# A chain of attention, expert and feed-forward layers on one core: attention-value product ahead of the last score unit, a DRAM fill in 22 pieces, norms in fused instructions, expert choice in three steps

## What is computed

```python
x = x + tanh(g_xattn[0]) * attention(layernorm(x), ctx, ctx)            # att0: 16 heads of 8, 512 keys
x = x + tanh(g_ffn[0])   * moe_top1(layernorm(x))                       # 8 experts, one per token, hidden 512
h = layernorm(x)
y = ln(h + attention(h, h, h), ln1_g, ln1_b)                            # att1: 256 keys
y = ln(y + attention(y, ctx, ctx), ln2_g, ln2_b)                        # att2: 512 keys
y = ln(y + relu(y @ fc1 + b) @ fc2 + b, ln3_g, ln3_b)                   # feed-forward
x = x + tanh(g_xattn[1]) * y
z = layernorm(x)
u = z + causal_attention(rmsnorm(z, g1), rope)                          # att3: 256 keys, 4 key heads
x = x + tanh(g_ffn[1])   * (u + moe_top2(rmsnorm(u, g2)))               # 4 experts, two per token
```

## Time and profile before

| | us |
|---|---|
| Median of three runs | 1365.55 |
| The three runs | 1375.97, 1365.55, 1359.68 |
| The profiled execution's own time | 1377.16 |
| Its span, first to last instruction | 1375.2 |
| TensorE busy | 1138.4 |
| VectorE busy | 789.1 |
| ScalarE busy | 593.9 |
| GpSimd busy | 391.3 |

### The profile page before, as it was taken

How to read it: one execution, slowest core, us unless ns; L and a number is a source line. 1 busy time by engine, 2 the same in 40 slices (tenths; PEclk the granted TensorE clock), 3 DMA queues, 4 the chain that set the end, 5 groups by cost and what they waited for, 6 DMA issues and landing times. The chain is left out here.

```text
span 1375.2 us, 24810 instructions
## 1 busy us (share of the span) xinstructions
PE 1138.4 (83%) x8548; PEld 674.0 (49%) x8548; DVE 789.1 (57%) x1887; ACT 593.9 (43%) x947; POOL 391.3 (28%) x1038
## 2 busy tenths in 40 slices
PE   2799889799888677787899988888888778788897
PEld 1245444377454465344444444434565556555554
DVE  2567776533766212567777758667575655534433
ACT  1266554445564333455455644534443333332121
POOL 2333222611344312454333324222242422100000
PEclk9999887799997789789899998988999988889999
DMA  8544333454335343556444434423343434201000
GB/s 229 152 120 134 113 111 112 148 160 120 96 115 163 94 135 106 148 152 208 152 146 146 144 98 126 130 84 97 93 138 109 144 100 135 63 17 39 8 23 8
DMA packets 173235, 158.72 MB, mean 115 GB/s; under 512 B 12681, under 2 KB 147209, under 8 KB 173065
## 3 DMA queue, kind: packets, MB, share of 16 engines
q1 hardware_dynamic: 168920, 142.02, 34.7%
q0 software_dynamic: 4192, 15.12, 3.5%
HBM read 91.56 MB, written 67.63 MB: 116 GB/s over the span
## 5 line engine op out<-in xcount | busy, mean ns | idle before, releaser
L1043 ACT ACTIVATE prob<-e_ps 128x1024 f32<-128x1024 f32 (+1 forms) x384 | 375.1, 988 | 233.6 <-PE e_ps L1555 157.3
L1202 DVE TENSOR_REDUCE nmax<-s_ps 128x1 f32<-128x512 f32 x512 | 331.5, 685 | 175.4 <-PE s_ps L1518 173.9
L1518 PE MATMUL s_ps<-Kst,Qst 72*128 72x512 bf16 x512 | 207.6, 422 | 68.0 <-DVE nmax L1202 51.1
L1555 PE MATMUL e_ps<-Qst,Kst 75*128 75x256 bf16 x1408 | 252.3, 295 | 13.2 <-DMA Qst<-mrow 4.6
L1571 PE MATMUL av_ps<-prob,Vx 128*32 128x256 f32 (+1 forms) x3072 | 229.1, 422 | 0.0
L1555 PEld LDWEIGHTS e_ps<-Qst,Kst 75*128 75x128 bf16 x1408 | 135.2, 104 | 124.9 <-issue 72.8
L967 POOL TENSOR_TENSOR mparts<-nmax,zeros 128x8 bf16<-128x8 f32 x128 | 26.7, 208 | 376.6 <-issue 363.9
L1571 PEld LDWEIGHTS av_ps<-prob,Vx 128*32 128x32 f32 x3072 | 87.0, 118 | 90.9 <-issue 59.2
L1046 ACT ACTIVATE OT<-av_ps 128x256 f32<-128x256 f32 x128 | 49.2, 384 | 179.6 <-PE av_ps L1571 179.5
L1211 DVE TENSOR_REDUCE nmax<-s_ps 128x2 f32<-128x512 f32 x128 | 85.2, 686 | 59.0 <-PE s_ps L1532 58.6
L1518 PEld LDWEIGHTS s_ps<-Kst,Qst 72*128 72x128 bf16 x512 | 52.9, 104 | 129.0 <-DVE nmax L1202 80.7
(11 more groups left out here) (193 smaller groups left out, 1679.5 us busy)
## 6 DMA issues: line engine op xcount, KB each, us to landing
q_parts<-qp SPq DMA_DIRECT2D x96, 192.0 KB, 2.4
k_parts<-kp SPq DMA_DIRECT2D x48, 384.0 KB, 3.3
Qst<-q_parts SPq DMA_DIRECT2D x128, 144.0 KB
Kst<-k_parts SPq DMA_DIRECT2D x64, 288.0 KB
k_parts<-kp SPq DMA_DIRECT2D x48, 192.0 KB, 2.6
Kst<-k_parts SPq DMA_DIRECT2D x64, 144.0 KB
ctxT<-in_ctxT SPq DMA_DIRECT2D x16, 256.0 KB, 4.6
FB<-xs_rows SPq DMA_DIRECT2D x22, 128.0 KB, 2.5
```

Of the source, the lines that this page charges most:

```text
L1043: act.activation(dst, src, ACT.Exp).then_inc(e_drained, 1)
L1202: ve.tensor_reduce(nmax[:, g, u, h % GH:h % GH + 1], s_ps[:, c % 2, :], AX.X, ALU.max, negate=True).then_inc(s_drained, 1)
L1518: last = pe.matmul(s_ps[:, c % 2, :], Qst[0:ROWS, par, s, u * P:u * P + P], Ks[0:ROWS, par, s, :], start=True, stop=True)
L1555: last = pe.matmul(o, Ks[0:KROWS, par, h, t * P:t * P + P], Qst[0:KROWS, par, h, :], start=True, stop=not a.rope)
```

## The change

1. **Order of the product.** In `body`, the AV piece of a slot stands ahead of the slot's last S unit instead of behind it (in slots with two units: E, first unit, small step, AV, second unit).
2. **Positions.** In att3 `maxT` goes from positions 5 and 9 to 4 and 8, `proj` from 11 to 10, `apply` from 14 to 12, and `v` from 10 to 12. In att1 and att2 `apply` is divided: `center` at 10 and the rest at 13, where it stood at 12.
3. **Norms.** (x - mean)*gain and then *rstd + shift, each one `scalar_tensor_tensor` per 128 x 128 tile; in att3 and `f.rms` x*rstd*gain in one. For att1 and att2 the first pair doesn't need `rstd`, so `center` runs before it is there. In the feed-forward `f.center` and `f.scale` replace `f.norm`, `f.gain` and `f.shift`.
4. **Choice.** `m0.choose` has three parts, at positions 5, 6 and 7 (for the last sequence of a half all at 12).
5. **Fill.** The zeros go out in 22 DMAs of 128 KB, at every second position from position 4 of problem 1 to position 14 of problem 3. The load of `m0c` goes from the start to position 5 of problem 0, with a semaphore of its own.

```diff
     it = {6: [("ctx", n, 0)], 7: [("ctx", n, 1)], 15: [("nT", n, None)]}
     if a.wo:
         it[8] = [("aT", n, None)]
-        it[11] = [("proj", n, None)]
-        it[14] = [("apply", n, None)]
+        it[10 if a.rope else 11] = [("proj", n, None)]
+        it[12 if a.rope else 14] = [("apply", n, None)]
     else:
         it[8] = [("resid", n, None)]
-        it[12] = [("apply", n, None)]
+        it[10] = [("center", n, None)]
+        it[13] = [("apply", n, None)]
...
-        put(n, 15, ("f.norm", i, None))
-        put(n + 1, 0, ("f.gain", i, None))
-        put(n + 1, 1, ("f.shift", i, None))
+        put(n, 15, ("f.center", i, None))
+        put(n + 1, 0, ("f.scale", i, None))
-        put(n + 1, 10, ("f.gain1", i, None))
...
+    put(0, 5, ("m0.const", 0, None))
+    for k in range(2 * NT):
+        put(1, 4 + 2 * k, ("m0.fill", k // NT, k % NT))
     for b in range(B):
         if b % HALF < HALF - 1:
-            for p, kind in ((3, "m0.gate"), (6, "m0.choose"), (9, "m0.rank")):
-                put(b + 2, p, (kind, b, None))
+            put(b + 2, 3, ("m0.gate", b, None))
+            for k in range(3):
+                put(b + 2, 5 + k, ("m0.choose", b, k))
+            put(b + 2, 9, ("m0.rank", b, None))
     for g in range(B // HALF):
         last = HALF * g + HALF - 1
         n = last + 1
-        for p, kind in ((11, "m0.gate"), (12, "m0.choose"), (13, "m0.rank")):
-            put(n, p, (kind, last, None))
+        put(n, 11, ("m0.gate", last, None))
+        for k in range(3):
+            put(n, 12, ("m0.choose", last, k))
+        put(n, 13, ("m0.rank", last, None))
...
-    put(5, ("maxT", n, 2))
-    put(9, ("maxT", n, 3))
+    put(4 if a.rope else 5, ("maxT", n, 2))
+    put(8 if a.rope else 9, ("maxT", n, 3))
...
-        put(10, ("v", n + 1, None))
+        put(12 if a.rope else 10, ("v", n + 1, None))
...
+        product = []
         if s >= a.gs:
-            units += [[("AV", n, (s // a.gs - 1, x))] for x in range(a.avs) if (x + 1) * a.gs // a.avs - 1 == s % a.gs]
+            product = [("AV", n, (s // a.gs - 1, x)) for x in range(a.avs) if (x + 1) * a.gs // a.avs - 1 == s % a.gs]
         elif n > lo:
             p = att(n - 1)
-            units += [[("AV", n - 1, (NG - 1, x))] for x in range(p.avs) if (x + 1) * a.gs // p.avs - 1 == s]
+            product = [("AV", n - 1, (NG - 1, x)) for x in range(p.avs) if (x + 1) * a.gs // p.avs - 1 == s]
+        if product:
+            units.insert(max(1, len(units) - 1), product)
...
+                elif kind == "m0.const":
+                    sp.dma_start(m0c[:, :], dram["m0c"]).then_inc(m0c_loaded, 16)
+                elif kind == "m0.fill":
+                    sp.dma_start(xs_rows[n][arg * TILE:(arg + 1) * TILE, :], dram["blank"]).then_inc(blank_stored, 16)
...
-            late(m0c[:, :], dram["m0c"])
             late(fc1b[:, :], dram["fc1b"])
             late(gw1[:, :], dram["gw1"])
-            for g in range(B // HALF):
-                blank = dram["blank"].unsqueeze(0).to_broadcast([NT, TILE, D])
-                sp.dma_start(xs_rows[g].rearrange("(n r) d -> n r d", r=TILE), blank).then_inc(blank_stored, 16)
...
-                    po.wait_ge(blank_stored, 16 * B // HALF)
+                    po.wait_ge(blank_stored, 16 * 2 * NT)
...
-                    act.wait_ge(late_loaded, LATE)
+                    act.wait_ge(m0c_loaded, 16)
...
+            def center_gain(L, dst, src, gain, t):
+                for i in range(t):
+                    ve.scalar_tensor_tensor(out=dst[:, i, :], in0=src[:, i, :], scalar=L["mv"][:, i, 0:1],
+                                            in1=vecs[:, VI[gain], :], op0=ALU.subtract, op1=ALU.mult)
+            def scale_shift(L, dst, src, shift, t):
+                for i in range(t):
+                    last = ve.scalar_tensor_tensor(out=dst[:, i, :], in0=src[:, i, :], scalar=L["rstd"][:, i:i + 1],
+                                                   in1=vecs[:, VI[shift], :], op0=ALU.mult, op1=ALU.add)
+                return last
+            def scale_rms(L, dst, src, gain, t):
+                for i in range(t):
+                    last = ve.scalar_tensor_tensor(out=dst[:, i, :], in0=src[:, i, :], scalar=L["rstd"][:, i:i + 1],
+                                                   in1=vecs[:, VI[gain], :], op0=ALU.mult, op1=ALU.mult)
                 return last
...
-            def one_hot(dst, src, e, tiles):
+            def one_hot(dst, src, e, tiles, part=None):
...
+                if part in (None, 0):
+                    ve.tensor_reduce(top, src, AX.X, ALU.max)
+                    ve.drain()
+                    ve.tensor_tensor(eq, src, top.unsqueeze(2).to_broadcast(bc), ALU.is_equal)
+                    ve.drain()
+                if part in (None, 1):
+                    ve.tensor_tensor(eq, eq, io, ALU.mult)
+                    ve.drain()
+                    ve.tensor_reduce(low, eq, AX.X, ALU.min)
+                    ve.drain()
+                if part in (None, 2):
+                    ve.tensor_tensor(dst, low.unsqueeze(2).to_broadcast(bc), io, ALU.is_equal)
+                    ve.drain()
...
+                elif kind == "center":
+                    ve.drain()
+                    center_gain(LA, tmp[:, 0:SQ].rearrange("p (t d) -> p t d", t=QT), newres[:, par, :, :],
+                                a.name + "_g", QT)
...
-                        t4 = tmp[:, SQ:2 * SQ].rearrange("p (t d) -> p t d", t=QT)
-                        apply_norm(LA, t3, newres[:, par, :, :], QT, rms=a.tail == "rms")
-                        ve.drain()
                         if a.tail == "rms":
-                            ve.tensor_tensor(dst, t3, over("att3_g", QT), ALU.mult).then_inc(norm_ready, 1)
+                            scale_rms(LA, dst, newres[:, par, :, :], "att3_g", QT).then_inc(norm_ready, 1)
                         else:
-                            ve.tensor_tensor(t4, t3, over(a.name + "_g", QT), ALU.mult)
-                            ve.drain()
-                            ve.tensor_tensor(dst, t4, over(a.name + "_b", QT), ALU.add).then_inc(norm_ready, 1)
+                            scale_shift(LA, dst, t3, a.name + "_b", QT).then_inc(norm_ready, 1)
...
-                    one_hot(ohs[:, j:j + QT, :], lg[:, 0:QT, :], E0, QT)
-                    ve.tensor_copy(ohb[:, :, :], ohs[:, j:j + QT, :]).then_inc(m0_chosen, 1)
+                    one_hot(ohs[:, j:j + QT, :], lg[:, 0:QT, :], E0, QT, arg)
+                    if arg == 2:
+                        ve.tensor_copy(ohb[:, :, :], ohs[:, j:j + QT, :]).then_inc(m0_chosen, 1)
...
-                elif kind == "f.norm":
+                elif kind == "f.center":
+                    ve.drain()
+                    center_gain(LF, f_res, f_res, "ffn_g", BT)
+                elif kind == "f.scale":
                     ve.wait_ge(f_rstd, f_stat(n, 0))
-                    apply_norm(LF, f_res, f_res, BT)
-                elif kind == "f.gain":
-                    ve.drain()
-                    ve.tensor_tensor(f_res, f_res, over("ffn_g", BT), ALU.mult)
-                elif kind == "f.shift":
-                    ve.drain()
-                    ve.tensor_tensor(f_res, f_res, over("ffn_b", BT), ALU.add)
+                    ve.drain()
+                    scale_shift(LF, f_res, f_res, "ffn_b", BT)
...
-                    apply_norm(LF, f_out, f_res, BT, rms=True)
-                elif kind == "f.gain1":
-                    ve.drain()
-                    ve.tensor_tensor(f_out, f_out, over("g1", BT), ALU.mult).then_inc(f_normed, 1)
+                    scale_rms(LF, f_out, f_res, "g1", BT).then_inc(f_normed, 1)
```

23 lines of the change are left out of this document (6 added, 17 removed).

## The result

| | before | changed |
|---|---|---|
| Median of four runs, us | 1370.76 | 1332.86 |
| Lowest and highest, us | 1359.68, 1378.32 | 1320.61, 1336.79 |
| Profiled execution: time, span, us | 1377.16, 1375.2 | 1336.79, 1335.0 |

The changed kernel is faster: ratio 0.9698, 95% interval 0.9645 to 0.9751. The forecast was 1307 us in a range of 1270 to 1350, a ratio of 0.957: the sign and the case are right, the gain is some 38 us instead of 58. A median takes in all executions of a kernel, a ratio and its interval only those within 1.5% of the fastest of the same kernel, so a ratio can differ from the quotient of two medians.

A forecast was written before the change was run, and what follows sets the result against it. TensorE was taken to lose about 237 us in gaps and to run 270 us at half speed. Fill 7.5, 31.4 for choice, product and att3, and clock 20 gave 58.9 us, a factor 0.957: 1307 us, range 1270 to 1350.

The forecast's parts named there:

- The fill, 7.5 us: At the start: without the zeros ahead of the k stores, K's reload and all behind it come 7.5 us earlier (4 to 10.4).
- The choice, 7.8 us: Spreading the choice over three slots closes two TensorE waits of 1.9 us and four of about 1: 7.8 us (3 to 11).
- The product, 13.2 us in att2 and 3 each in att0 and att1: AV ahead of the last unit pays where VectorE has a burst before that unit: 19 us in all (0 to 25).
- a plain pair gains nothing: Two att2 slots without small steps but `maxT`: after the product moves, the wait is as long, only elsewhere.
- 0.85 of the 1.65: Per att2 problem, E comes 0.85 us earlier at slots 10 and 11 because AV starts before the unit that waited.
- att3, 15 us: New att3 positions save 1.2 us in five light problems and 3.1 in three with a choice: 15 us (-12 to 24).
- Three quarters: A closed wait partly opens at the next resource, so 31.4 of the 41.8 us of choice, product and att3 were kept.
- the last three terms: Choice 7.8, product 19 and att3 15 us, together 41.8 us before the reduction to 31.4.
- The clock, 20 us: TensorE: 45 of 270 us at half speed go, mostly behind choices and long `nT` waits, at 0.45 each: 20 us (-20 to 60).
- The signs: Expected in the trace: first unit at 32 to 34 us, no 1.88 us wait, units' waits about 35, clock 0.92 or more.
- The product pays nothing: Rival: moving AV only puts the same wait in another place; 25.5 us gained in all, 1340 us; chance 0.22.
- two-tensor operations in SBUF: Rival: each fused norm operation takes twice 348 ns, costing 20 us on VectorE in its busiest slots: 1327 us; chance 0.02.

The follow-up runs named there:

- the version with the big fill: Changed kernel with the zeros in two DMAs of 1.44 MB, issued at positions 4 and 6 of problem 1, instead of 22 small ones: 1338.5 us, ratio 0.9751.
- `apply` under a product: Changed kernel with att0's and att3's `apply` at 13, and in att1 and att2 `resid` at 9 and `center` at 11: 1305.69 us, ratio 0.9572.
- the kernel with `apply` at 12: Kernel before plus moved product and fused, split norms, with the norm's second part in att1 and att2 at 12 instead of 13: 1350.6 us, ratio 0.9890.

## Why the prediction was right, and where its sizes were off

- *The fill, 7.5 us.* Right: the k stores are issued in 1.6 us, K's reload stands at 29.09 (I had 27.9 to 29.4), the first unit 7.2 us earlier. By nT0 it is 10.8, of which the fill alone gives 8.7.
- *The choice, 7.8 us.* The number came out in part by luck: 8.1 us alone, of which 4.1 are gaps, and I had counted gaps only. In the full change att0 gains 4.9; the next point says why.
- *The product, 13.2 us in att2 and 3 each in att0 and att1.* From v to `nT` of att2 the working held: 11.7 us in seven stretches, 1.67 each, where I had 1.65. Six of the seven lie between nT15 and nT23 and give 9.5 us; att2 gained 9.1. What I had as "a plain pair gains nothing" missed that `maxT` and the product run side by side, 0.30 us per pair. The step that failed is "att0 and att1, which keep most of their bursts (`proj`, `resid`), 3 each by the 0.2 and two pairs". I had looked for bursts in front of a second unit that the moved product would cover, and not for bursts that the product at the end of a slot had covered so far. TensorE's gaps in att0 are 32.0 us without the order and 40.9 with it (42.8 in the version with the big fill); the order alone takes them from 36.4 to 39.7. In problems 2 and 3, where the choices stand, it is plainest: 68.6 us without the order, 72.6 and 72.8 with it in those two kernels, and 68.7 with `apply` under a product, with gaps of 5.5, 9.3, 9.4 and 8.6 us. So the order added gaps; `apply` under a product gave little of them back, and took away the half speed behind them (8 us in the changed kernel, none there). In the length of att0 the loss shows in the full set (290.4 without, 296.1 with, 293.2 with the big fill) and not in the kernel before (301.1 without, 297.6 with), so it isn't a settled number. att1 shows no gain by the order in any pair. And 0.85 of the 1.65 was put down to the product by itself; alone it doesn't give it.
- *att3, 15 us.* Right in size, and partly by luck. Of the 14.5 us, 10.8 are gaps, and I had counted gaps only; the rest goes with 13 us less of half speed, which was in another term. The working also has a slip: the light problems' `nT` wait of 2.07 against a new one of 2.5 is -0.4, not -0.2, so by its own steps the sum is near 14. The new wait of `maxT` for v's copies was forecast as 2.5 to 3.8 us in each of eight; it came as 11.6 us in six, while the `nT` wait fell to 2.1.
- *Three quarters.* The parts of the last three terms came to 4.9 + 0.8 + 9.1 + 14.5 = 29.3 us, half-speed changes included, against 31.4.
- *The clock, 20 us.* The largest miss. I let 45 of 270 us of half speed go; 19 went. The price per slow microsecond was near (0.36 and 0.50 against 0.45), so at that price the term is worth 7 to 10 us, and even these lie inside the 29.3 and the 10.8 above. By the clock to three places, att0 lost some 14 us of half speed, att2 7 and att3 13, but att1 got 17 more. The step that failed is that the slow stretches behind removed waits would be gone; others came where a wait had grown or moved, as behind the 1.21 us at `resid`.
- *The signs.* First unit, the wait of 1.88, the `nT` wait and its successor came as written, and an att2 problem at full clock takes 29.7 us, not 32. The units' waits did not: 47.9 us instead of about 35. The mean clock was 0.906 to 0.922 in the four executions, not 0.92 or more.
- *The rivals.* "The product pays nothing" is refuted for the whole change (0.977 without the order, 0.970 with it; in att2 10.7 us), and by itself it paid less than nothing (1.018). For these tiles two-tensor operations in SBUF are not slow: the groups of the fused norm take what the earlier trace rows show for one operand.

```profile
L1171 DVE SCALAR_TENSOR_TENSOR tmp<-newres,la_mv,vecs 128x128 f32<-128x128 f32 x32 | 10.0, 354 | 1.8 <-issue 0.4
L1177 DVE SCALAR_TENSOR_TENSOR normed<-tmp,la_rstd,vecs 128x128 f32<-128x128 f32 x32 | 9.8, 349 | 1.5
```

354 and 349 ns against 348 for the one-source form with two scalars per row (with one, `L1155` of the kernel before, it is 286). The Trainium skill's rule ("VectorE: DVE Perf Modes", section "The perf-mode tier table") puts two-tensor operations on float32 in SBUF at half the rate of one-source ones, in a table for 2048 elements. If that held for the whole of an instruction of 128, they would take some 700 ns, an estimate; the trace doesn't agree for these shapes.

What the changed kernel's gain consists of, in short: 10.8 us at the start, 14.5 in att3, 9.1 in att2 by order and norms together, 4.9 in att0 (the choice and less half speed, less what the order costs there), next to nothing in att1. These are the profiled executions' numbers, with the scatter named above. Not settled: why the order alone runs at a lower clock in most of its executions, why att1's clock varies as it does from kernel to kernel, and with it how much of a local gain arrives at the end.

## What to carry to other kernels

When a long step is moved ahead in a fixed order, look at both sides of it: which waits it will now cover, and which bursts of the other engine stood behind it and were covered so far; move those with it. Parts of such a change can't be judged one by one: here five parts multiply to 1.015 and give 0.970 together. Where the clock differs between executions, read a part's effect from stretches between the same events, and its worth from repeated times.

## What the runs showed of the hardware that was not expected

- Two waits of 0.70 and 0.69 us with a product between them left the clock at its upper level; one of 1.47 us at the same place was followed by 6 us at 0.59. That the wait brings the fall isn't shown, though: of the waits of 1.2 to 1.6 us at `maxT` of slot 9, those at 745.25 (changed kernel) and in the kernel with order and norms (first pair below) had half-speed matmuls behind them, and those of the kernel with `apply` at 12 (second pair) and of the order alone (1.22 us, at 763.96) had not.

```profile
757.02 0.39 PE L1531 MATMUL s_ps<-Kst,Qst 72*128 72x512 bf16 x1 [1.58 <-DVE nmax L1221]
...
759.75 1.06 PE L1568 MATMUL e_ps<-Qst,Kst 75*128 75x256 bf16 x4
```

```profile
749.24 0.39 PE L1531 MATMUL s_ps<-Kst,Qst 72*128 72x512 bf16 x1 [1.58 <-DVE nmax L1221]
...
750.86 0.60 PE L1568 MATMUL e_ps<-Qst,Kst 75*128 75x256 bf16 x4
```

- The time of one and the same kernel follows its mean clock: 0.905 and 1371.4 us, 0.893 and 1389.7 for the order alone; 0.906 and 1336.8, 0.922 and 1320.6 for the changed kernel.
- `maxT` (12 columns of weights) and the product (32 columns) behind it run side by side: the product's first matmul starts 0.01 us after `maxT`'s, and the pair takes 1.07 us to the next unit, where apart they took 0.28 and 1.01.
